# Second layer's expert results scattered by token tile by tile, residual rows and layernorm chains taken many heads early

## The chip, the cores and the metric

The kernel runs on one core of a Trainium2 chip. The metric is the device time of one execution in microseconds: 466.25 us is the median of three runs of the kernel before (465.55 to 466.74). The engines are TensorE (PE), VectorE (DVE), ScalarE (ACT), GpSimd (POOL) and SyncE (SP), each with its own in-order queue; they meet through semaphores.

## The reference

`x` is 1024 tokens of 256 channels (4 batches of 256), `ctx` has the same batches.

```python
x = x + xattn0(layernorm(x), ctx)     # activations per 1x128 and weights per 128x128 block
                                      # brought to an 8-bit grid, then x_q @ ctx_q.T
x = x + ffn0(layernorm(x), ...)       # 32 experts of width 192, top 4, softmax of the top, x 1.8,
                                      # plus one shared expert
x = x + xattn1(layernorm(x), ctx, gamma)  # 8 heads of 32 channels over 256 positions, softmax
x = x + ffn1(layernorm(x), ...)       # 8 experts of width 176, top 2, shares out of a full softmax,
                                      # plus a shared expert of width 352
```

## The kernel before, in words

Tokens lie in 8 tiles of 128 rows (`NT`), token tile t being `x_sb[:, t]`. Five parts follow one another.

**Start (0 to 49 us).** DVE takes the statistics of the layernorm, ACT normalises (L529 to L535). The context is scaled and rounded on DVE (L746 to L751) and POOL forms `wq` from it with one addition and one subtraction over 2048 columns (L436 to L438). DVE takes the largest value of each 128-block of the normalised x (L755), forms `rin_x` (L757 to L759), multiplies x by it (L761 to L763), and rounds in two halves (L769 to L773). PE multiplies, and DVE adds into `x_sb` (L778).

**First mixture of experts (layer m0, routing 49 to 94 us, tiles to 243.6 us).** The router chooses, one-hot matrices give each 128-row tile's list of tokens (`tab`), and for m0 also where each result row belongs (`dest`, L861 to L869: matmuls L1192, then `kth`). While the routing waits, ACT, POOL and PE work off four shared-expert steps (`early_shared`, `shared_steps`): POOL multiplies (L456) and adds the result to `x_sb` (L461), and DVE's tile loop begins only when all four are added (L923, L971). Then come 48 tiles of two 64-row blocks (`tiles`): POOL gathers rows (L482), ACT and DVE copy the second block's weights, PE does gate/up, transposes and down. POOL scatters each tile's rows to token-ordered homes in DRAM (`home`, L472), and SP loads them back, 512 KB for each token tile (L383).

**Second attention (243.6 to about 341 us).** `take(t)` adds the four weighted rows of each token of tile t into `x_sb` (L947, four operations in a chain). `queries(tiles)` then takes statistics and the reciprocal deviation on DVE, a chain of small linked operations (L303 to L313), scaled for the queries, and ACT normalises. The 32 heads go in 16 pairs, four heads to a token tile. PE does `scores` of a pair, DVE takes maxima (`head_max`, L979), ACT exponentiates (L646), PE turns the probabilities (`turn_p`, L1314), ACT copies them (L654), and after each tile's four heads PE does `values` (L1325, L1333), DVE `tile_out` (L990 to L994). PE's order is written out: turn pair p, scores of pair p+2, and for every second p the values of a tile. The orders on DVE and ACT are written out too: `takes` says before which head DVE takes which tile, `by_pair` at which head it makes which pair of tiles' queries, `by_pool` at which heads the deviation of the next layernorm goes to POOL (`deviations`), to be used by DVE three heads later.

**Second mixture of experts (m1: routing 341 to 366 us, tiles to 427.5 us).** The same with 20 tiles. SP stores every tile's result as it is (L351 to L353); at the end POOL gathers by token, 16 gathers for 8 token tiles and 2 choices (`gather_back`, L492), by way of the slots in `back` (L836).

**Last (427.5 us to the end).** Fifteen shared-expert steps remain (`after_shared`), and for the last eight DVE adds the routed rows (`combine`) and SP stores the output.

## Time and profile before

| | us |
|---|---|
| median of 3 runs | 466.25 |
| the profiled execution: device time | 468.48 |
| its span, first to last instruction | 466.4 |
| around the span (launch and end) | 2.08 |
| PE busy | 356.5 (76%) |
| DVE busy | 280.5 (60%) |
| ACT busy | 201.7 (43%) |
| POOL busy | 164.5 (35%) |
| mean granted clock of PE | 0.908 of full |

The shares are averages over parts with different limits. PE's granted clock is given as a share of full speed, 1.00 (2.4 GHz) or 0.50 (1.2 GHz); a mean between the two is a stretch with a change in it. "Issue" in the chain is time in which the engine waited for nothing that the profile shows.

### The profile page before, as it was taken

To read this page: it belongs to the slowest core of one execution; us is meant where nothing else is said; L and a number is where in the kernel's file an instruction comes from. 1 tells how busy PE (TensorE), PEld (TensorE's weight loads), DVE (VectorE), ACT (ScalarE), POOL (GpSimd) and SP (SyncE) were. 2 spreads that over 40 slices of the span, in tenths; PEclk is the share of its full clock that TensorE was granted. 3 is DMA by queue.
4 is the path that set the end of the run, shared out by engine and by line. 5 is a ranking of instruction groups with operands and counts; after the bars stand their busy time and mean duration, and the time that the engine had idled before them with its cause. 6 is when DMAs were issued, how large, how long until landed. Compare 5 with 4: busy or idle time off the path is not lost.

```text
span 466.4 us, 8276 instructions
## 1 busy us (share of the span) xinstructions
PE 356.5 (76%) x2359; PEld 203.0 (44%) x2359; DVE 280.5 (60%) x791; ACT 201.7 (43%) x467; POOL 164.5 (35%) x220
## 2 busy tenths in 40 slices
PE   0003397789999999999983665667766899998996
PEld 0002184435555545555442444444554345444664
DVE  3999859645555555555558639395877155554365
ACT  1301245255555555555413737355731355554221
POOL 2060204756666666666310000002310533300560
PEclk9999998999999999999995558596985699999999
DMA  8999970094222322345557930000002223321232
GB/s 236 353 302 271 341 192 0 23 298 128 91 91 91 91 92 92 92 106 172 164 183 296 272 107 3 0 1 0 4 3 88 69 91 92 94 68 45 80 114 79
DMA packets 28780, 57.32 MB, mean 123 GB/s; under 512 B 3825, under 2 KB 13937, under 8 KB 28737
## 3 DMA queue, kind: packets, MB, share of 16 engines
q1 hardware_dynamic: 20785, 38.38, 27.0%
q0 software_dynamic: 6336, 17.31, 12.7%
q10 hardware_dynamic: 1616, 1.11, 0.8%
q8 instruction: 21, 0.34, 0.3%
q14 instruction: 22, 0.18, 0.1%
HBM read 44.72 MB, written 12.06 MB: 122 GB/s over the span
## 4 chain that ended last, share of the span: by engine, by line
PE 66%; DVE 18%; issue 8%; ACT 3%; POOL 2%; DMA 2%; DVEq 0%; ACTq 0%; SPq 0%; POOLq 0%
PE bank L1226 19%; PE bank L1253 13%; PE bank L1100 5%; PE bank L1237 5%; PE bank L1302 4%; PE bank L1217 3%; PE bank L1111 3%; PE bank L1314 3%; PE bank L1151 2%; PE bank L1089 2%; DMA x_sb<-x 2%; DVE x_sb L947 1%; DVE att_nm L979 1%; PE bank L1333 1%; DVE st L704 1%
## 5 line engine op out<-in xcount | busy, mean ns | idle before, releaser
L1226 PE MATMUL bank<-arena,xT 128*64 x272 | 112.5, 496 | 1.3 <-ACT xT L608 1.3
L1229 PE MATMUL bank<-xn,xT 128*64 128x384 f32 (+1 forms) x272 | 112.5, 497 | 0.0
L482 POOL DMA_INDIRECT xg<-m_xn,tab x68 | 65.7, 967 | 61.3 <-PE bank L1217 52.5
L1253 PE MATMUL bank<-arena,hT 96*64 (+1 forms) x272 | 70.4, 381 | 1.9 <-DVE hT L906 1.3
L1256 PE MATMUL bank<-xn,hT 96*64 96x256 f32 (+1 forms) x272 | 70.4, 381 | 0.0
L601 ACT ACTIVATE xn<-arena 128x768 f32 (+1 forms) x68 | 56.3, 827 | 21.9 <-issue 21.8
L931 DVE TENSOR_TENSOR hh<-sg,bank 128x192 f32<-128x192 f32 (+1 forms) x71 | 24.8, 350 | 63.0 <-ACT sg L624 63.0
L474 POOL DMA_INDIRECT m_ys<-ysb,dest x48 | 47.4, 988 | 23.9 <-issue 12.8
L1253 PEld LDWEIGHTS bank<-arena,hT 96*64 96x64 f32 (+1 forms) x272 | 34.8, 135 | 38.7 <-issue 28.2
L608 ACT ACTIVATE xT<-bank 128x256 f32<-128x256 f32 x71 | 27.2, 383 | 47.8 <-PE bank L1217 47.1
L1302 PE MATMUL bank<-arena,xn 32*128 32x256 f32 x128 | 23.0, 521 | 27.7 <-issue 21.4
L900 DVE COPY xn<-arena 96x512 f32 (+1 forms) x68 | 28.8, 423 | 23.7 <-issue 23.7
L1226 PEld LDWEIGHTS bank<-arena,xT 128*64 128x64 f32 x272 | 31.8, 138 | 23.7 <-issue 14.6
L303 POOL TENSOR_SCALAR ve<-mv 128x2 f32<-128x2 f32 (+1 forms) x4 | 0.8, 194 | 110.1 <-DVE mv L707 110.1
L979 DVE TENSOR_REDUCE att_nm<-bank 128x2 f32<-128x512 f32 x32 | 21.4, 685 | 26.8 <-PE bank L1302 26.6
L624 ACT ACTIVATE sg<-bank 128x192 f32<-128x192 f32 (+1 forms) x71 | 23.2, 326 | 32.7 <-PE bank L1229 30.1
L918 DVE COPY ysb<-bank 128x256 f32<-128x256 f32 x68 | 28.9, 425 | 14.0 <-PE bank L1256 9.1
L646 ACT ACTIVATE arena<-bank,att_nm 128x256 f32<-128x256 f32 x64 | 29.7, 473 | 14.9 <-DVE att_nm L979 14.8
L1256 PEld LDWEIGHTS bank<-xn,hT 96*64 96x64 f32 (+1 forms) x272 | 34.8, 135 | 0.0
L1100 PE MATMUL bank<-arena 128*128 128x352 f32 (+1 forms) x84 | 33.2, 523 | 0.0
L1229 PEld LDWEIGHTS bank<-xn,xT 128*64 128x64 f32 x272 | 31.9, 138 | 0.0
L530 ACT ACTIVATE xn<-x_sb,nmr,rstd 128x256 f32<-128x256 f32 x24 | 12.7, 590 | 43.5 <-DVE nmr L740 35.2
(173 smaller groups left out, 615.2 us busy)
## 6 DMA issues: line engine op xcount, KB each, us to landing
arena<-w_gu SPq DMA_DIRECT2D x3, 3456.0 KB, 18.8
arena<-w_dn SPq DMA_DIRECT2D x3, 1728.0 KB, 24.5
arena<-m_ys SPq DMA_DIRECT2D x8, 512.0 KB, 5.5
m_ys<-ysb SPq DMA_DIRECT2D x20, 128.0 KB, 1.7
arena<-w_gu SPq DMA_DIRECT2D x2, 1056.0 KB
m_xn<-xn SPq DMA_DIRECT2D x2, 1024.0 KB, 6.4
arena<-w_gu SPq DMA_DIRECT2D x1, 1408.0 KB
arena<-w_gu SPq DMA_DIRECT2D x1, 1152.0 KB, 11.5
```

Source lines behind the costliest of these rows:

```text
L474: nc.gpsimd.indirect_dma_start(out=ys_d[L.name], out_offset=bass.IndirectOffsetOnAxis(ap=dest[:, s:s + 1], axis=0), in_=ysb[:, s % BUFS, : ...
L482: nc.gpsimd.indirect_dma_start(out=xg[:, b, :], out_offset=None, in_=xn_d[L.name], in_offset=bass.IndirectOffsetOnAxis(ap=d["tab"][:, s:s ...
L601: nc.scalar.activation(second[L.name][0][:, s % 2, :], arena[:, bass.ds(off, L.gu)], ACT.Copy).then_inc(m["gu_second"], 1)
L646: nc.scalar.activation(pr_sb[:, g % 4, q, :], bank[g % 4][:, q * H:(q + 1) * H], ACT.Exp, bias=nm[:, g % 4, q:q + 1], accum_out=sum_sb[:, ...
L900: V.tensor_copy(second[L.name][1], arena[0:L.J, bass.ds(off + L.gu, 2 * H)]).then_inc(m["dn_second"], 1)
L918: V.tensor_copy(ysb[:, s % BUFS, :], bank[6 + s % 2][:, 0:H]).then_inc(m["y_copied"], 1)
L1100: ins = T.matmul(bank[4 + n % 2][:, 0:2 * J2], RS[L.name]["xT"][:, t, c, :], arena[:, at:at + 2 * J2], start=(c == 0), stop=(c == C - 1))
L1226: T.matmul(bank[2 + s % 2][0:BLOCK, 0:2 * J2], xT[:, s % 2, c, 0:BLOCK], arena[:, bass.ds(off + c * 2 * J2, 2 * J2)], start=(c == 0), stop ...
L1229: return T.matmul(bank[2 + s % 2][BLOCK:P, 0:2 * J2], xT[:, s % 2, c, BLOCK:P], gu2[:, s % 2, cols], start=(c == 0), stop=(c == C - 1), ti ...
L1253: T.matmul(bank[6 + s % 2][0:BLOCK, 0:H], hT[0:L.J, s % 2, a, 0:BLOCK], arena[0:L.J, bass.ds(off + L.gu + a * H, H)], start=(a == 0), stop ...
L1256: ins = T.matmul(bank[6 + s % 2][BLOCK:P, 0:H], hT[0:L.J, s % 2, a, BLOCK:P], dn2[:, a * H:(a + 1) * H], start=(a == 0), stop=(a == 1), ti ...
L1302: ins = T.matmul(bank[g % 4][:, q * H:(q + 1) * H], xn[rows, t, q * P:(q + 1) * P], k_sb[rows, t, :], start=True, stop=True, tile_position ...
```

## The change

Four edits go together.

1. Start: the product x times `rin_x` moves from DVE to ACT, 16 operations of 128 columns; `wq` moves from POOL to DVE, its addition ahead of the rounding, its subtraction between the two halves.
2. Early shared steps: POOL does the multiplications only; its four additions into `x_sb` are made in the tile loop, one ahead of each of the gathers 4 to 7. ACT writes the four results to four buffers. DVE's tile loop waits for an addition only where it writes over that buffer.
3. Attention: tiles 0 and 1 have their queries made together, tiles 2 and 3 are taken before the first head, tiles 4 to 7 before heads 1, 2, 6 and 7. The deviations of the queries from tile 2 on, and of the next layernorm, are made by POOL: `chains` says at which head DVE gives the statistics, for which tiles, whether for queries, and at which head they are used.
4. Second layer: results go to token-ordered homes as in the first layer, with `kth`, `dest` and the matmuls for them, and are loaded back by SP. PE's tiles wait for `dest_ready`. The SP stores and the 16 gathers at the end go.

```diff
-        by_pair = {4: (2, 3), 12: (4, 5), 19: (6, 7)}
-        by_pool = {22: (0, 1), 24: (2, 3), 28: (4, 5)}
+        chains = [(-1, (2, 3), True, 2), (2, (4, 5), True, 7), (7, (6, 7), True, 12),
+                  (11, (0, 1), False, 15), (19, (2, 3), False, 23), (27, (4, 5), False, 31)]
@@ sync
-                    if L is L1:
-                        sp.dma_start(ys_d[L.name][s * P:(s + 1) * P, :],
-                                     ysb[:, s % BUFS, :]).then_inc(m["y_stored"][s % BUFS], 16)
...
             store_tiles(L1)
+            rows_of_tokens(L1)
@@ gpsimd
-            pool.wait_ge(c_mag, 1)
-            link(nc.gpsimd.tensor_tensor(v_c, v_c, c_c, ALU.add))
-            nc.gpsimd.tensor_tensor(wq.rearrange("p b k n -> p (b k n)"), v_c, c_c, ALU.subtract).then_inc(wq_ready, 1)
...
+            def early_add(L, n):
+                q, t = M[L.name]["early"], early_work[L.name][n][1]
+                pool.wait_ge(q["y_copied"], n + 1)
+                nc.gpsimd.tensor_tensor(x_sb[:, t, :], x_sb[:, t, :], ysb[:, n, :], ALU.add).then_inc(q["added"], 1)
...
                         pool.wait_ge(m["t_done"], s - BUFS + 1)
+
+                        if s - BUFS < n_early[L.name]:
+                            early_add(L, s - BUFS)
...
-                    if L is L0 and s >= ahead:
+                    if s >= ahead:
                         home(s - ahead)
...
             def deviations(i):
+                _, tiles, asked, _ = chains[i]
+                a, b = tiles[0], tiles[-1] + 1
                 pool.wait_ge(stats_ready, i + 2)
-                inverse_deviation(nc.gpsimd, link, by_pool[sorted(by_pool)[i]], 1.0)
-                pool.sem_inc(rstd_ready, 1)
+                inverse_deviation(nc.gpsimd, link, tiles, SCALE if asked else 1.0)
+                link(nc.gpsimd.tensor_tensor(nmr[:, a:b], mv[:, a:b, 0], rstd[:, a:b], ALU.mult))
+                nc.gpsimd.tensor_scalar(nmr[:, a:b], nmr[:, a:b], -1.0, None, ALU.mult).then_inc(rstd_ready, 1)
@@ scalar
+            act.wait_ge(rin_ready, 1)
+            for a in range(16):
+                block_of = v_x[:, a * P:(a + 1) * P]
+                nc.scalar.activation(block_of, block_of, ACT.Copy, scale=rin_x[:, a:a + 1]).then_inc(xs_ready, 1)
...
-            queries(1, [0])
-            softmax_exp(0)
-            softmax_exp(1)
-            queries(2, [1])
-            softmax_exp(2)
+            act.wait_ge(chain_ready, 1)
+            for t in range(2):
+                normalise(t, q_ready)
+            for g in range(3):
+                softmax_exp(g)
...
-                if g in by_pair:
-                    queries(3 + sorted(by_pair).index(g), by_pair[g])
+                for i, (_, tiles_of, asked, turn) in enumerate(chains):
+                    if asked and turn == g:
+                        act.wait_ge(rstd_ready, i + 1)
+                        for t in tiles_of:
+                            normalise(t, q_ready)
@@ vector
-            link(V.scalar_tensor_tensor(out=amx[:], in0=amx[:], scalar=ACT_EPS, in1=amx[:], op0=ALU.max, op1=ALU.max))
+            link(V.tensor_scalar(amx[:], amx[:], ACT_EPS, None, ALU.max))
             link(V.reciprocal(rin_x[:], amx[:]))
-            link(V.scalar_tensor_tensor(out=rin_x[:], in0=rin_x[:], scalar=FP8_MAX, in1=rin_x[:], op0=ALU.mult, op1=ALU.max))
-            n = NT * H // 2
-            for i in range(2):
-                v16 = v_x[:, i * n:(i + 1) * n].rearrange("p (a n) -> p a n", n=P)
-                V.tensor_tensor(v16, v16, rin_x[:, 8 * i:8 * i + 8].unsqueeze(2).broadcast_to([P, 8, P]), ALU.mult)
+            V.tensor_scalar(rin_x[:], rin_x[:], FP8_MAX, None, ALU.mult).then_inc(rin_ready, 1)
+
+            link(V.tensor_tensor(v_c, v_c, c_c, ALU.add))
...
+                dve.wait_ge(xs_ready, 8 * (i + 1))
                 link(power_of_two(c, v))
                 link(V.tensor_tensor(v, v, c, ALU.add))
                 V.tensor_tensor(qx[:, i * n:(i + 1) * n], v, c, ALU.subtract).then_inc(xq_ready, 1)
+                if i == 0:
+                    V.tensor_tensor(wq.rearrange("p b k n -> p (b k n)"), v_c, c_c, ALU.subtract).then_inc(wq_ready, 1)
...
             take(0)
-            queries([0])
             take(1)
-            head_max(0)
-            head_max(1)
-            queries([1])
-            head_max(2)
-            head_max(3)
-
-            takes = {3: 2, 4: 3, 9: 4, 12: 5, 16: 6, 19: 7}
+            queries([0, 1])
+            take(2)
+            take(3)
+            statistics(chains[0][1]).then_inc(stats_ready, 1)
+            for g in range(4):
+                head_max(g)
+
+            takes = {1: 4, 2: 5, 6: 6, 7: 7}
             for g in range(nheads):
                 if g in takes:
                     take(takes[g])
-                if g in by_pair:
-                    queries(by_pair[g])
-                if g in by_pool:
-                    statistics(by_pool[g]).then_inc(stats_ready, 1)
-                if g - 3 in by_pool:
-                    dve.wait_ge(rstd_ready, sum(k <= g - 3 for k in by_pool))
-                    normalise(by_pool[g - 3], M["m1"]["xn_ready"])
+                for i, (given, tiles_of, asked, turn) in enumerate(chains):
+                    if given == g:
+                        statistics(tiles_of).then_inc(stats_ready, 1)
+                    if turn == g and not asked:
+                        dve.wait_ge(rstd_ready, i + 1)
+                        normalise(tiles_of, M["m1"]["xn_ready"])
@@ tensor
             routing(L1, rw1, (w1_in, 96), 2)
+            pe.wait_ge(dest_ready, 2)
             tiles(L1)
```

`rows_of_tokens(L)` is the loop of L383 to L388 made for either layer: eight loads, each from the fifth on waiting for the one four before it.

## Rows read from the trace of the kernel before

**Rows 1.** The page: shares by engine of the chain that ended last.
```profile
PE 66%; DVE 18%; issue 8%; ACT 3%; POOL 2%; DMA 2%; DVEq 0%; ACTq 0%; SPq 0%; POOLq 0%
```

**Rows 2.** Stretches: length, engines' busy us (instructions), clock, DMA share, GB/s.
```profile
243.60:341.00 97.40, 58.70 (x484) 39.09 (x484) 63.77 (x188) 53.53 (x170) 8.74 (x42) 0.70 0.28 87
366.00:427.50 61.50, 58.90 (x401) 28.31 (x402) 30.23 (x81) 31.95 (x63) 16.81 (x18) 0.96 0.28 83
427.50:466.40 38.90, 33.89 (x140) 22.12 (x140) 19.30 (x48) 9.75 (x28) 15.15 (x16) 1.00 0.29 85
```

**Rows 3.** Chain of waits in order of time: start us, us, what.
```profile
251.59 0.70 DVE att_nm L979
...
264.41 7.69 issue
...
288.21 7.04 issue
...
312.48 5.58 issue
```

**Rows 4.** Timeline 0 to 60 us: start, us, engine, line, operation, count, idle before.
```profile
16.63 4.04 ACT L530 ACTIVATE xn<-x_sb,nmr,rstd 128x256 f32<-128x256 f32 x8 [11.84 <-DVE nmr L740]
...
22.18 4.50 POOL L437 TENSOR_TENSOR arena<-arena 128x2048 f32<-128x2048 f32 x1 [18.36 <-DVE arena L727]
24.33 2.39 DVE L757 SCALAR_TENSOR_TENSOR amx<-amx 128x16 f32<-128x16 f32 x1
...
26.76 4.50 POOL L438 TENSOR_TENSOR arena<-arena 128x2048 bf16<-128x2048 f32 x1
27.04 4.25 DVE L759 SCALAR_TENSOR_TENSOR rin_x<-rin_x 128x16 f32<-128x16 f32 x1
31.32 2.36 DVE L763 TENSOR_TENSOR xn<-xn,rin_x 128x1024 f32<-128x1024 f32 x2
...
34.31 0.69 DVE L726 TENSOR_SCALAR arena<-xn 128x1024 int32<-128x1024 int32 x1
...
35.76 1.23 DVE L772 TENSOR_TENSOR xn<-xn,arena 128x1024 f32<-128x1024 f32 x1
```

**Rows 5.** Timeline of DVE, 262 to 318 us: a take and a pair's queries.
```profile
265.94 1.99 DVE L947 SCALAR_TENSOR_TENSOR x_sb<-arena,rw,x_sb 128x256 f32<-128x256 f32 x4
267.97 0.75 DVE L704 BATCH_NORM_STATS2 st<-x_sb 128x6 f32<-128x256 f32 x2
...
269.04 0.17 DVE L303 TENSOR_SCALAR ve<-mv 128x2 f32<-128x2 f32 x1
...
271.21 0.16 DVE L740 SCALAR_TENSOR_TENSOR nmr<-mv,rstd 128x2 f32<-128x2 f32 x1
```

**Rows 6.** Stretches of the attention, columns as in Rows 2.
```profile
256.50:264.40 7.90, 7.90 (x32) 5.38 (x32) 3.51 (x7) 6.81 (x25) 0.00 (x0) 0.50 1.05 296
...
272.10:278.50 6.40, 6.40 (x48) 4.19 (x48) 1.29 (x2) 2.41 (x8) 0.00 (x0) 0.50 0.26 57
...
323.00:338.00 15.00, 12.02 (x132) 8.27 (x131) 10.95 (x29) 11.72 (x38) 6.88 (x33) 1.00 0.01 3
```

**Rows 7.** Timeline of PE: turned probabilities of the twelfth and sixteenth pair.
```profile
322.79 1.14 PE L1314 MATMUL bank<-ident,arena 128*128 128x128 f32 x8
...
336.49 1.09 PE L1314 MATMUL bank<-ident,arena 128*128 128x128 f32 x8
```

**Rows 8.** Timeline, last deviations on POOL and DVE behind them.
```profile
335.99 0.19 POOL L303 TENSOR_SCALAR ve<-mv 128x2 f32<-128x2 f32 x1 [3.13 <-DVE mv L707]
...
339.86 0.19 POOL L313 TENSOR_TENSOR rstd<-nt,rstd 128x2 f32<-128x2 f32 x1
340.21 0.73 DVE L712 TENSOR_SCALAR xn<-x_sb,mv,rstd 128x256 f32<-128x256 f32 x2 [2.19 <-POOLq L510]
```

**Rows 9.** The page: the scatter of the first layer, busy us, mean ns, idle before.
```profile
L474 POOL DMA_INDIRECT m_ys<-ysb,dest x48 | 47.4, 988 | 23.9 <-issue 12.8
```

**Rows 10.** One line of the kernel: ns min/median/max, first and last start.
```profile
L866 DVE SCALAR_TENSOR_TENSOR kth<-bank,kth x3: 207/207/208, 89.0 to 89.4; 128x48 f32<-128x48 f32 x3
```

More of the change, by code:

```diff
@@ L223, in mk_xattn_ffn @@
         xn_d = {L.name: nc.dram_tensor(L.name + "_xn", (n_tok, H), F32, kind="Internal").ap() for L in (L0, L1)}
-        homes = (n_tok + 1) * L0.K
-        ys_d = {L.name: nc.dram_tensor(L.name + "_ys", (L.tiles * P + (homes if L is L0 else 0), H), F32, kind="Internal").ap()
-                for L in (L0, L1)}
+        homes = (n_tok + 1) * max(L0.K, L1.K)
+        ys_d = {L.name: nc.dram_tensor(L.name + "_ys", (homes + L.tiles * P, H), F32, kind="Internal").ap() for L in (L0, L1)}
         batch_in = [sem(f"batch_in{b}") for b in range(NB)]
@@ L291, in mk_xattn_ffn @@
         n_early = {"m0": 4, "m1": 1}
+        assert max(n_early.values()) <= BUFS
         n_mid = {"m0": 1, "m1": 1}
@@ L364, in store_tiles, with rows_of_tokens @@
                     sp.wait_ge(m["y_stored"][b], 16 * (L.tiles // BUFS))
+            def rows_of_tokens(L):
+                for t in range(NT):
+                    if t >= 4:
+                        sp.wait_ge(*returned(L, t - 4))
+                    at = (t * P + 1) * L.K
+                    sp.dma_start(back_rows[L.name][:, t], ys_d[L.name][at:at + P * L.K, :].rearrange(
+                        "(p k) h -> p k h", k=L.K)).then_inc(returned(L, t)[0], 16)
             sp.wait_ge(ctxT_in, 16)
@@ L517, in _ @@
             gathers(L1)
-            gather_back(L1)
         @block.scalar
@@ L655, in pT_copy @@
                                      ACT.Copy).then_inc(pT_ready, 1)
-            def queries(n, tiles):
-                act.wait_ge(chain_ready, n)
-                for t in tiles:
-                    normalise(t, q_ready)
-            queries(1, [0])
-            softmax_exp(0)
-            softmax_exp(1)
-            queries(2, [1])
-            softmax_exp(2)
+            act.wait_ge(chain_ready, 1)
[3 more added lines that the diff above has]
+                softmax_exp(g)
             for g in range(nheads):
@@ L917, in y_copy @@
                         dve.wait_ge(m["y_stored"][s % BUFS], 16 * (s // BUFS))
+                    elif s < n_early[L.name]:
+                        dve.wait_ge(m["early"]["added"], s + 1)
                     V.tensor_copy(ysb[:, s % BUFS, :], bank[6 + s % 2][:, 0:H]).then_inc(m["y_copied"], 1)
@@ L922, in tiles @@
                 dve.wait_ge(m["table_e"], m["nth"])
-                dve.wait_ge(m["early"]["added"], n_early[L.name])
                 every_tile = L.tiles + len(last_work[L.name])
```

104 lines of the change are left out of this document (35 added, 69 removed).

## Prediction

> **What bounds the kernel now.** I read the shares of the chain that ended last first: PE holds 66% of it, DVE 18%, and 8% is "issue", time in which PE stood still for a reason the profile doesn't name [rows 1]. Then the busy times by stretch. The second layer's tiles are PE's (58.9 us busy of 61.5, clock 0.96), and so is the end (33.9 of 38.9, clock 1.00). The attention isn't: in 97.4 us PE is busy for 58.7, DVE for 63.8, ACT for 53.5, and the clock is 0.70 on average [rows 2]. The chain in order of time says where this goes: PE stands still for 7.69, 7.04 and 5.58 us, each time ahead of scores [rows 3]. DVE's timeline has the reason: a take of 1.99 us, then the queries' statistics and chain from 267.97 to 271.37, 3.4 us in which DVE takes no maxima and ACT has nothing to normalise [rows 5]. So the attention is bound by what the order on DVE puts in front of the scores.
>
> I write all times on the axis of the profile before, and shift at the end.
>
> **Start.** Two operations of 16 columns, L757 and L759, take 2.39 and 4.25 us on DVE. They end when POOL's L437 and L438 end (22.18 + 4.50 and 26.76 + 4.50) [rows 4]: while POOL worked, DVE stood. With `wq` off POOL they cost what small operations cost, about 0.2 each [rows 10]. Now step by step. The reduction has ended at 24.33; two small operations and a reciprocal bring `rin_x` at 25.0. DVE then adds for `wq` over 2048 columns, twice the 1.23 of 1024 columns: 27.5, and makes `dq`, 0.6: 28.1. ACT meanwhile scales 8 blocks. Eight normalisations of 256 columns took 4.04 [rows 4]; half the columns cost at most that and at least half. I take 3.0: 28.0, in time. The first half's rounding is 2 x 0.70 + 2 x 1.25 = 3.9: 32.0. Then the subtraction for `wq`, 2.4, and the second half, 3.9: 38.3, where before it ended at 42.1 (34.31 + 2 x 3.9). ACT's second eight blocks hide under this. **-3.8 us**. Bounds: -2.7 if a block costs a full 0.5 (8 blocks end at 29.1), -4.1 if everything small is free.
>
> **Early shared steps.** POOL's four additions leave the routing for the tile loop. POOL's multiplications come out of the order sooner only if an addition was in front of one. DVE's stretch there is busy with 16-bit comparisons, and it should lose less to POOL. I take **-0.3**, bounds -0.8 and 0. In the tile loop POOL does an addition ahead of each of four gathers; it has four buffers' lead there, and scatters begin only with the eighth tile. Cost 0; if DVE's copies are held each time for one addition (a 2048-column operation is 4.50 [rows 4], an eighth is 0.6) and nothing takes it up, +2.4.
>
> **Attention.** First maximum before: 251.59 [rows 3]. Changed, from 243.6: two takes 4.0, one chain for two tiles 3.4, two more takes 4.0, statistics 1.1 [rows 5]: 256.2. That is 4.6 us later. The first turned probabilities follow 1.7 us on (a maximum of 0.7 [rows 3], an exponential of about 1): 257.9. The first pairs have no values. Two such pairs took 7.90 us at clock 0.50, 32 matmuls [rows 6], so 3.95 each. Pairs 0 and 1 end at 265.8. During this DVE has takes 4 and 5, statistics and the maxima of the fourth pair to do (2.0 + 2.0 + 1.1 + 1.3), which cannot all be hidden: I give 1 us. With pair 2's turns and scores 270.8. Values and pair 3 are one stretch of 48 matmuls, 6.4 us at 0.50 [rows 6]: 277.2. Now DVE alone holds PE: a maximum 0.7, tile-out 1.4, take 2.0, statistics 1.1, a maximum 0.7 = 5.9 us (take 6 was hidden before). 283.1; values at the upper level, 1.5: the sixth pair is turned at 284.6.
> From here no take is left, the queries' chains run on POOL, and only light work stands on DVE. POOL's chain took 335.99 to 340.05 for 14 linked operations [rows 8], 0.29 each; 16 take 4.6 us. Chain 1 is given at head 2 and used at head 7, chain 2 given at 7 and used at 12: five heads of 1.7 us each, 8.5 us, so neither is waited for. The rate is that of the last stretch before, in which DVE had no takes either: twelfth pair at 322.79, sixteenth at 336.49 [rows 7], four pairs in 13.7 us, 3.4 a pair at clock 1.00. Ten pairs: 34.3. The sixteenth pair is turned at 318.9 instead of 336.5: **-17.6 us**. The same from the other side: three stalls of 20.3 go [rows 3], and with them two returns of the clock to 0.50 that cost some 3 each; the later start takes back 4.6, the new wait 3 to 4.
> Bounds: ten pairs at 3.1 and no wait at the sixth pair give -24; at 3.7, with the clock at 0.50 again after the wait, -11.
>
> **End of the attention.** DVE waited 2.19 us for POOL's last deviations, and the last tile's values behind it [rows 8]. Given at head 27 instead of 28 the chain begins about 1.4 earlier and is 0.55 longer: **-0.9**, bounds -1.5 and +0.5.
>
> **Second routing.** Added: eight matmuls of 20 columns (eight of 128 take 1.14 [rows 7]; I take 0.3) and three DVE operations in a chain, 0.21 each [rows 10]. One copy (`back`) goes. DVE's multiplication for the shared step is queued behind them, and PE's next transposes wait for it; the gather of the first tile, issued before, lands under this. **+0.5**, bounds 0.2 and 1.5. That `dest_ready` is waited for on PE costs no more, as DVE has `dest` 2 us before PE arrives there.
>
> **Second layer's tiles.** POOL now has a gather and a scatter for each tile: 2 x 0.99 [rows 9] and 0.3 of issue behind each, 2.6 us. A tile takes 61.5 / 20 = 3.1 us, fill included [rows 2]. It fits; the first layer runs so. 0, and +4 if the scatter's landing is waited for (0.2 a tile). SP's stores were hidden, so nothing is gained.
>
> **Last stretch.** The 16 gathers go and eight loads of 256 KB come. 2 MB at 296 GB/s [rows 6] are 7 us; from 431 they have landed by 438 to 440, and the first is wanted after eight of the sixteen steps' times, at about 447 (427.5 + 8 x 2.4). PE bounds it as before [rows 2]. 0.
>
> **Sum.** -3.8 - 0.3 - 17.6 - 0.9 + 0.5 = -22.1 us. The profiled execution took 468.48 us (span 466.4 and 2.08 around it), so 446.4 for such a one; it lies 2.2 above the median of 466.25, and on the median's footing the result is **444.2 us**.
>
> **Rivals.**
> *The clock falls back in the new wait.* My walk has PE idle for 3 to 4 us before the sixth pair. Against: nothing but a short wait, and pairs run dense before it. For: after the stalls of 7.04 and 5.58 PE began again at 0.50. A pair with values takes 6.4 there against 3.4 and 1.5, and two pairs pass until it rises: +3 to +3.5, and if it happens twice +6.5: 447.5 to 450.7. 25%.
> *The clock rises early.* What the rows show: in 256.5 to 264.4 PE is busy for 7.90 of 7.90 us and the clock stays at 0.50; in the next busy stretch, with values in it, it rises after 6.4 us [rows 6]. If it rose in the first pairs, pair 2, values and pair 3 would take about 6 us instead of 11.4; DVE would then be the bound and give back 1.8: 440.6. 12%. The Trainium skill ("TensorE: Matmul & The Clock Gate", Why this matters for your kernels) says to keep TensorE busy without gaps to get it past the slow state; by that rule this rival is the forecast, at 440.6. The busy 7.90 us at 0.50 here speak against it.
> *The stall only moves.* Takes, statistics or POOL's chains come late, DVE holds the scores for some 4 to 8 us more, or the scatters are waited for in the second layer: 448 to 452. 8%.
> *Slower.* The takes and the waits of ACT for POOL leave PE just enough gaps that it never leaves 0.50 between 244 and the second layer's tiles. Two pairs are then 3.95 + 6.4 = 10.4 us, ten pairs 52 instead of 34.3: +17.7; the end of the attention and the second routing add 4, the pairs before 2. -22.1 + 23.7 = +1.6: 467.9. It decides from nine pairs of ten on. Against: in all three busy stretches with values the clock rose. 5%.
> My own case has 50%.
>
> **Range and chances.** 8 in 10: from 438 (the attention's upper bound shared with the early rise) to 454. The measurement tells 0.3%, 1.4 us, from no change. Faster 0.94, the same 0.02, slower 0.04 (the slower case lies at the very edge, so a part of its 5% counts as the same).
>
> **What would show it.** L757's and L759's successors under 0.3 us, the rounding's end at 38; the first maximum 4 to 5 us later behind the last m0 tile; no stall over 5 us after it, and at most one of 3 to 4 before the values of the second tile; PE's clock over 0.85 in the attention's second half; POOL's chains without a wait on ACT; 20 tiles in 61 to 62 us with 20 scatters on POOL. I am wrong if the clock stays at 0.50 in the pairs from the sixth on, or if maxima wait behind something other than a take.

## The result, and the profile after

The changed kernel takes 452.44 us (median of 4 runs, 451.57 to 453.46) where the kernel before took 466.5 beside it: ratio 0.9694, 95% interval 0.9655 to 0.9732. Run again later beside the experiments it took 452.93 us, ratio 0.9673 (0.963 to 0.9715). The prediction was 444.2 us, the range 438 to 454. The direction and the place of the gain are right, its size is not: the profiled execution went from 468.48 to 452.69 us (span 450.4), 15.8 us where 22.1 were predicted. The other 2 of the 8 us are a matter of footing: the profile before lay 2.2 us above its median, the one after 0.25. The medians here and below are over all runs; the ratios leave out a run more than 1.5% above its kernel's fastest (one each of "takes spread" and "second layer's scatter undone" below).

The page's shares of the chain answer to [rows 1]. PE has gained a point, issue has fallen from 8% to 5%:
```profile
PE 67%; DVE 19%; issue 5%; ACT 3%; POOL 3%; DMA 2%; DVEq 0%; SPq 0%; ACTq 0%; POOLq 0%
```
Stretches of the changed kernel, with the columns of [rows 2]. The first is the attention (97.0 us from about the first take, about as long as before), the next two are the second layer's tiles and the last stretch:
```profile
241.00:338.00 97.00, 65.45 (x564) 44.84 (x564) 65.85 (x203) 56.26 (x176) 20.41 (x97) 0.77 0.32 99
350.00:411.50 61.50, 59.39 (x401) 28.35 (x401) 30.31 (x79) 31.95 (x63) 36.50 (x38) 0.95 0.27 83
411.50:450.40 38.90, 33.98 (x142) 22.17 (x140) 19.32 (x48) 9.75 (x28) 0.96 (x1) 0.97 0.26 85
```
The last two are what they were (58.90 and 33.89 us of PE before). In the first, PE does 564 matmuls where it did 484, at clock 0.77 instead of 0.70: the work is denser, and a part of the second routing's falls in it now.

The start, timeline (start, us, engine, line): the two small operations are free of GpSimd, and the rounding ends at 37.5 where it ended at 42.1:
```profile
23.89 0.17 DVE L739 TENSOR_SCALAR amx<-amx 128x16 f32<-128x16 f32 x1
24.38 0.17 DVE L741 TENSOR_SCALAR rin_x<-rin_x 128x16 f32<-128x16 f32 x1
24.59 4.78 ACT L522 ACTIVATE xn<-xn,rin_x 128x128 f32<-128x128 f32 x16 [4.36 <-DVE rin_x L741]
...
36.26 1.23 DVE L755 TENSOR_TENSOR ysb<-xn,arena 128x1024 bf16<-128x1024 f32 x1
```
They took 2.39 and 4.25 us in [rows 4], now 0.17 each. Their form has changed too, but one of the old form over 48 columns takes 0.21 [rows 10], so it is GpSimd's absence that counts.

The attention is where the rest lies. PE multiplies with the reciprocals of the softmax sums at the start of each tile's values. One line for each tile but the first, with the wait in front of it in brackets:
```profile
278.94 1.08 PE L1305 MATMUL bank<-ident,arena 128*32 128x128 f32 x16 [3.61 <-DVE arena L968]
288.74 0.64 PE L1305 MATMUL bank<-ident,arena 128*32 128x128 f32 x16 [1.75 <-DVE arena L968]
296.49 0.64 PE L1305 MATMUL bank<-ident,arena 128*32 128x128 f32 x16 [0.77 <-DVE arena L968]
303.92 0.64 PE L1305 MATMUL bank<-ident,arena 128*32 128x128 f32 x16 [1.42 <-DVE arena L968]
312.70 0.64 PE L1305 MATMUL bank<-ident,arena 128*32 128x128 f32 x16 [1.48 <-DVE arena L968]
320.13 0.64 PE L1305 MATMUL bank<-ident,arena 128*32 128x128 f32 x16 [2.48 <-DVE arena L968]
325.04 0.64 PE L1305 MATMUL bank<-ident,arena 128*32 128x128 f32 x16 [1.95 <-DVE arena L968]
```
No stall of 5 to 8 us is left, of which there were three [rows 3]; in their place stands a wait of 0.8 to 3.6 us in every tile, 13.5 us in seven. Each time it is for the reciprocal on DVE (L968). The sixteenth pair is turned at 321.56 instead of 336.49 [rows 7]. (A pair counts from the start of its first turn.)

Why DVE is late with them is seen in the chain of waits, in order of time (start us, us, what), from the second scores of a tile on:
```profile
283.63 1.32 PE bank L1282 x8
284.95 0.67 DVE att_nm L961
285.62 0.40 DVE arena L972
286.05 0.43 DVE arena L974
286.50 0.44 DVE x_sb L976
286.96 0.76 DVE st L687 x2
...
288.49 0.20 DVE arena L968
```
At step 10 of its loop DVE gets the scores of head 14 at 284.95, takes one maximum (L961), then writes out the tile before (L972 to L976), takes statistics (L687), takes another maximum, and only then forms reciprocals (L968) whose sums had long been there. It had itself been idle for 4.89 us ahead of that maximum, waiting for PE. The two engines wait for each other in turn.

The clock, over the wait at 278.94 and over the ten pairs behind it:
```profile
276.00:284.00 8.00, 5.06 (x42) 3.40 (x44) 3.90 (x11) 3.87 (x14) 3.19 (x16) 0.57 0.01 3
281.70:321.60 39.90, 30.81 (x317) 20.70 (x313) 22.19 (x54) 29.21 (x98) 8.72 (x44) 0.93 0.00 1
```
It did fall back in the new wait, to 0.50 from 277 to 284, and once more from 304.5 to 307.9. A second profile of the same kernel (the run "changed, again" below) has the first fall too (279.5 to 282.9), but then two others, 289.7 to 293.2 and 320.5 to 323.9, and none at 304. Its ten pairs took 38.7 us.

Second routing, added operations: three of 0.18 us on DVE. PE waits 0.94 us for DVE's multiplication behind them (0.52 before), but later 0.54 us for the first tile's gather to land, so the gather sets the time:
```profile
346.32 0.18 DVE L845 SCALAR_TENSOR_TENSOR kth<-bank,spare 128x20 f32<-128x20 f32 x1
...
346.75 0.18 DVE L850 SCALAR_TENSOR_TENSOR dest<-bank,kth 128x20 uint32<-128x20 f32 x1
346.85 0.33 DVE L861 TENSOR_TENSOR hh<-sg,bank 128x176 f32<-128x176 f32 x1
...
350.03 0.66 PE L1197 MATMUL bank<-ident,xg 128*128 128x128 f32 x2 [0.54 <-DMA xg<-m_xn,tab]
```

### The profile page after: what moved, and what is told of

Its sections match the earlier page's. It is cut to its first block, busy times and chain, and to the rows that moved or that the text cites. A ratio compares the mean times of both kernels' runs of the same rounds, so it can differ in the third digit from the quotient of the medians.

```text
span 450.4 us, 8288 instructions
## 1 busy us (share of the span) xinstructions
PE 354.4 (79%) x2367; PEld 202.0 (45%) x2367; DVE 267.2 (59%) x745; ACT 205.7 (46%) x483; POOL 168.0 (37%) x276
## 4 chain that ended last, share of the span: by engine, by line
PE 67%; DVE 19%; issue 5%; ACT 3%; POOL 3%; DMA 2%; DVEq 0%; SPq 0%; ACTq 0%; POOLq 0%
PE bank L1206 21%; PE bank L1233 13%; PE bank L1081 6%; PE bank L1217 5%; PE bank L1092 4%; PE bank L1197 4%; DVE x_sb L930 3%; PE bank L1294 2%; PE bank L1282 2%; PE bank L1132 2%; DVE st L687 2%; DVE att_nm L961 2%; DMA x_sb<-x 2%; PE bank L1070 1%; PE bank L1313 1%
## 5 line engine op out<-in xcount | busy, mean ns | idle before, releaser
L466 POOL DMA_INDIRECT m_ys<-ysb,dest x68 | 67.0, 986 | 38.8 <-DVE ysb L902 22.0
L914 DVE TENSOR_TENSOR hh<-sg,bank 128x192 f32<-128x192 f32 (+1 forms) x71 | 24.8, 349 | 62.4 <-ACT sg L609 62.4
L593 ACT ACTIVATE xT<-bank 128x256 f32<-128x256 f32 x71 | 27.2, 384 | 47.9 <-PE bank L1197 47.8
L609 ACT ACTIVATE sg<-bank 128x192 f32<-128x192 f32 (+1 forms) x71 | 23.2, 327 | 32.7 <-PE bank L1209 30.2
L961 DVE TENSOR_REDUCE att_nm<-bank 128x2 f32<-128x512 f32 x32 | 20.7, 673 | 23.4 <-PE bank L1282 22.1
L1217 PEld LDWEIGHTS bank<-ident,hh 128*96 128x96 f32 (+1 forms) x142 | 12.2, 125 | 41.0 <-issue 37.9
L1217 PE MATMUL bank<-ident,hh 128*96 128x128 f32 (+1 forms) x142 | 29.8, 292 | 0.3 <-DVE hh L914 0.3
```

The source lines that it names most:

```text
L466: nc.gpsimd.indirect_dma_start(out=ys_d[L.name], out_offset=bass.IndirectOffsetOnAxis(ap=dest[:, s:s + 1], axis=0), in_=ysb[:, s % BUFS, : ...
L961: V.tensor_reduce(nm[:, g % 4, :], bank[g % 4][:].rearrange("p (q k) -> p q k", q=2), AX.X, ALU.max, negate=True).then_inc(nm_ready, 1)
L1217: ins = T.transpose(bank[4 + s % 2][0:L.J, a * P:(a + 1) * P], hh[:, s % 2, a * L.J:(a + 1) * L.J], ident[:])
```

## Experiments

Each is the changed kernel with one edit (the last two rows join several), timed five to ten times beside the kernel before. Differences to the changed kernel are taken between ratios (its own is 0.9673) times 468 us. An interval is about 0.4% to either side, that of a difference about 0.6%, 2.2 to 3.2 us. So five lines differ clearly from the changed kernel: start, attention, chains on DVE, the two edits together and, barely, the last. Against its first measurement, 0.9694, every difference would read 1.0 us lower.

The last column has the attention's length in the one profile of each, from the first take to the last normalisation. It leaves out what happens before and behind, and in the five profiles with an unchanged attention (the first two rows, additions, scatter and the first profile) it lies between 90.4 and 92.2 us.

| kernel | median us | ratio (95%) | to the changed one, us | attention, us |
|---|---|---|---|---|
| changed, again | 452.93 | 0.9673 (0.963 to 0.9715) | | 90.4 (first profile 91.2) |
| start undone | 458.11 | 0.978 (0.9753 to 0.9806) | +5.0 | 91.8 |
| attention's order undone | 464.54 | 0.9919 (0.9886 to 0.9952) | +11.5 | 103.4 (kernel before 104.7) |
| additions undone | 451.21 | 0.963 (0.9608 to 0.9652) | -2.0 | 91.7 |
| second layer's scatter undone | 453.27 | 0.9667 (0.9631 to 0.9703) | -0.3 | 92.2 |
| chains on DVE, early takes kept | 460.72 | 0.9858 (0.9816 to 0.9901) | +8.7 | 98.4 |
| filler ahead of the values | 450.18 | 0.962 (0.9584 to 0.9657) | -2.5 | 90.1 |
| filler ahead of the attention | 451.95 | 0.9647 (0.9619 to 0.9674) | -1.2 | 91.7 |
| reciprocals early | 450.60 | 0.964 (0.96 to 0.968) | -1.5 | 89.1 |
| takes spread | 450.23 | 0.9607 (0.9554 to 0.966) | -3.1 | 87.7 |
| reciprocals early, takes spread | 448.81 | 0.9586 (0.9549 to 0.9622) | -4.1 | 85.8 |
| both, and additions undone | 450.41 | 0.9617 (0.959 to 0.9644) | -2.6 | 86.4 |

### Which part brings what

**The changed kernel again.**

> The changed kernel itself once more, beside which the other experiments are to be read. On its first chip its ratio to the kernel before was 0.9694 (0.9655 to 0.9732). If that holds here: 0.967 to 0.971; the variants with one part undone would then read as +4.0 us (start), +10.5 (attention), -3.0 (additions) and -1.3 (scatter). If the ratio is lower on other chips (0.963 to 0.966), the last two are no difference, start and attention are worth 1 to 3 us more each, and the reciprocals moved alone and the filler are worth little.

Its ratio is 0.9673, between the two cases. The additions and the scatter are then within the error, start and attention are worth 5.0 and 11.5 us. The four parts undone add up to 14.2 us, the whole change is worth 15.3 on the same footing.

**The start undone.**
```diff
+ link(nc.gpsimd.tensor_tensor(v_c, v_c, c_c, ALU.add))
+ nc.gpsimd.tensor_tensor(wq..., v_c, c_c, ALU.subtract)
- nc.scalar.activation(block_of, block_of, ACT.Copy, scale=rin_x[:, a:a + 1])
+ V.tensor_tensor(v16, v16, rin_x[...].broadcast_to([P, 8, P]), ALU.mult)
```


> The changed kernel with the start as before: the conversion of ctxT (add and subtract over 2048 columns) on GpSimd again, no scaling by ACT, scaling by DVE. Theory (the start was worth 4.6 us by the traces, and 2.0 us of that were lost again in the first routing, because TensorE's clock fell there to 0.50 at another place): 452.4 + 2 to 4.6 = 454.5 to 457.0 us; the two 16-column operations on DVE take 2 to 4.5 us again, the first expert tile begins some 3 us later. If the clock does not fall at the gate matmuls here, the time is at the low end, 454.5 to 455.5, and the 2.0 us belong to the start's new timing. Rival (the 2.0 us come from the moved additions and would be lost with the old start too): 456.5 to 457.0, and the stretch from the rounding's end to the first expert tile is as long as in the changed kernel (about 53 us).

+5.0 us, so the start is worth what its trace shows (4.6), within the error. The two operations take 2.39 and 4.25 us again. The first expert tile's first matmul comes at 95.39 us, 4.8 later than in the changed kernel's first profile (90.58); the low end of the theory is out, and so is that the new timing of the start costs 2 us. The rival's sign is met, 53.6 us from the rounding's end to the first expert tile; whether the additions are the reason is the next experiment's question.

**The additions undone.**
```diff
- if s - BUFS < n_early[L.name]: early_add(L, s - BUFS)
...
+ nc.gpsimd.tensor_tensor(x_sb[:, t, :], x_sb[:, t, :], ysb[:, (n - 1) % 2, :], ALU.add)   # in early_shared
```


> The changed kernel with the early shared steps' additions in the first and second routing again (on GpSimd between its multiplications), not in the tile loop. In the traces so far the stretch from the first counting matmul to the first expert tile is 22.9 us with these additions (kernel before) and 24.3 to 24.8 without them (three kernels), though DVE's one-hot operations are faster without. Theory 1 (moving the additions costs: without them TensorE's gate matmuls of the shared steps follow at another time and stand at clock 0.50 longer, up to 2.77 us for a set that takes 1.46 otherwise): this kernel is faster than the changed one by 1 to 2 us, 450.5 to 451.5, the stretch 22.5 to 23.2 us. Theory 2 (the clock falls there from run to run whatever the order): 452.0 to 453.0, the stretch about 24.3. Theory 3 (my prediction, the move gains 0.3): 452.7.

Theory 1 fails in the trace: the stretch from the counting matmul (66.46) to the first expert tile (90.77) is 24.3 us with the additions back, not 22.5 to 23.2. Theory 2 stands as to the stretch, though the time, 451.21 us, is theory 1's. The sets of four gate matmuls take 1.46 us or up to 2.77, nearly twice that. In two profiles of the same changed kernel they are, first profile and then second:
```profile
68.70 2.48 PE L1081 MATMUL bank<-arena 128*128 128x384 f32 x4
74.01 1.46 PE L1081 MATMUL bank<-arena 128*128 128x384 f32 x4
```
```profile
69.44 2.76 PE L1081 MATMUL bank<-arena 128*128 128x384 f32 x4
74.71 2.77 PE L1081 MATMUL bank<-arena 128*128 128x384 f32 x4
```
Over all profiles of the changed kernel and its variants the stretch is 23.2, 24.3 or 24.8 us, in the kernel before 22.9; with the additions back it was 24.3 once and 23.2 once, so their place doesn't decide it. (The granted clock's own row reads 1.00 from 70 to 80 us in the second profile, so that the clock slows them there isn't shown.) By its ratio this kernel is 2.0 us faster than the changed one, but the intervals overlap, and in the last experiment the same edit brought nothing.

**The second layer's scatter undone.**
```diff
+ if L is L1: sp.dma_start(ys_d[L.name][s * P:(s + 1) * P, :], ysb[:, s % BUFS, :])
+ nc.gpsimd.indirect_dma_start(out=back_rows[L.name][:, t, k, :], ..., in_=ys_d[L.name], ...)   # 16, behind the last tile
- home(s), rows_of_tokens(L1), kth and dest for L1
```


> The changed kernel with the second layer's results stored tile by tile by SP and gathered back for each token, as before (no scatter, no kth and dest in the second routing, 16 gathers behind the last tile). Theory (by the traces the second routing changed by 0.0, the tiles by +0.2 and the combination by nothing, because TensorE is the bound of the last stretch and the gathers were in time): 452.4, from 451.7 to 453.0. Rival (the scatters cost in the tiles what the saved gathers bring at the end, or the other way round, by 1 us): 451 or 453.5.

-0.3 us: no difference, though the rival's 1 us either way would not show. In the traces the tiles take 56.6 us without the scatter and 57.2 with it, and the last stretch 43.2 in both (43.2 and 44.8 in the changed kernel's two profiles): PE bounds both stretches that this part touches.

**The attention's order undone.**
```diff
- takes = {1: 4, 2: 5, 6: 6, 7: 7}
+ takes = {3: 2, 4: 3, 9: 4, 12: 5, 16: 6, 19: 7}
...
+ if g in by_pair: queries(by_pair[g])               # by_pair = {4: (2, 3), 12: (4, 5), 19: (6, 7)}
```


> The changed kernel with the order of the attention as before (tokens taken at heads 3, 4, 9, 12, 16, 19, the queries' chains on DVE in front of maxima, GpSimd's three chains late). Theory (the attention is where the gain is: 12.3 us to the last turned pair and 1.1 at its end): 452.4 + 13.4 = 465.8 us, 464.5 to 467, and three stalls of TensorE of 5 to 8 us ahead of scores are back. Rival (part of the gain comes from the earlier start or from nothing in the order, for instance from where the clock happens to rise): 458 to 462.

+11.5 us, somewhat less than the 13.4 of the traces. The three stalls are back (7.69, 7.04 and 5.34 us in its chain), and with them the low clock, the fives in the middle of this line (a digit for each fortieth of the span, in tenths of full speed):
```profile
PEclk9999998899999999999995569586976799999998
```
Its ten runs lie from 461.95 to 468.21 us, and the one profiled took 462.91, so its trace shows the order's cost at the low end.

**The early takes kept, the chains back on DVE.**
```diff
- statistics(tiles_of).then_inc(stats_ready, 1)          # chain follows on GpSimd
...
+ link(statistics(tiles_of)); inverse_deviation(V, link, tiles_of, SCALE); negated_means(...)
```


> The changed kernel with the queries' chains of tiles 2 to 7 (three times some 2.5 us of small linked operations) on DVE again, at the same heads, with the early takes kept: so only GpSimd's share of the change is taken away. Theory (both count: the early takes put the work ahead of and into the first pairs, the chains on GpSimd keep 2.4 us out of each of three places on DVE; at the start of the attention and at heads 2 and 7 nothing hides them): +2.4 for the first maximum, and 2.4 to 3 more at the take of tile 7, where TensorE already waits 3.6 us: in all 5 to 7 us slower than the changed kernel. Rival (the early takes alone are the gain, since DVE has slack in the first pairs at clock 0.50): 1 to 3 us slower, the first maximum late by 2.4 and the rest hidden.

+8.7 us, above the theory's 5 to 7 by less than the error, and far from the rival. In its trace the first maximum comes 2.4 us later behind the first take (14.96 against 12.59), and the whole attention takes 98.4 us, 7.2 to 8.0 more than in the changed kernel's two profiles. PE's wait ahead of the sixth pair, 3.61 us in the changed kernel, is now:
```profile
285.31 1.08 PE L1311 MATMUL bank<-ident,arena 128*32 128x128 f32 x16 [6.29 <-DVE arena L968]
```
So of the 11.5 us in the attention most hangs on the chains that GpSimd has taken over; the early takes alone bring about 3, hardly more than the error (5.0 in the last column of the table, 103.4 against 98.4). Late takes with the chains on GpSimd were not run, so how far the two need each other is open. A linked operation costs GpSimd 0.29 us and DVE 0.20, and it still pays: PE, DVE and ACT wait for one another in a ring of scores, maxima, exponentials and turns, and GpSimd stands outside it.

### Why a pair takes 4.0 us and not 3.4

**Reciprocals one head earlier.**
```diff
- if g % HPT == HPT - 1: head_inverses(g // HPT)
+ if g % HPT == HPT - 2: head_inverses(g // HPT)     # ahead of tile_out
```


> The changed kernel, only the reciprocals of a tile's sums stand one head earlier on DVE: ahead of the third head's tile-out, take and statistics and not behind them. Theory (the ten pairs took 4.0 us and not 3.4 because TensorE waits for these reciprocals before each tile's values, 13.5 us in seven waits; behind them ACT is next, with 2 x 0.47 + 2 x 0.2 for the exponentials and 0.6 for a copy, 1.75 a head, 3.5 a pair): ten pairs in 35 to 36.5 us, 452.4 - 4 = 448.5, from 447.0 to 449.5; TensorE's waits for the reciprocals fall under 4 us in all and the clock does not fall in the second half. Rival 1 (the ring of scores, maxima, exponentials and turns is what sets the pace, the reciprocals only end a wait that would be there anyway): the waits move to the turns, ten pairs stay at 39 to 40 us, 451.5 to 452.5. Rival 2 (the clock): the same time as far as it still falls twice.

The waits for the reciprocals are gone altogether (13.5 us to 0), yet the time falls by 1.5 us only, which the error covers, and the ten pairs took 39.8 us. Theory and rival 1 are each right in half: a part of the wait has moved. The sixteenth pair does come 3.6 us earlier (317.99 against 321.56, though this execution's first take was 0.9 later); at the last normalisation 1.3 is left of it (330.94 against 332.21), as DVE waits 1.60 us for GpSimd's last chain, which starts only 1.3 us earlier. The chain of waits of this kernel:
```profile
278.19 0.50 DVE x_sb L930
278.70 0.76 DVE st L687 x2
...
279.66 0.67 DVE att_nm L961
...
281.37 0.50 ACT arena L639
...
282.00 0.63 PE bank L1294 x4
282.63 1.83 PE bank L1282 x8
284.46 1.90 PE bank L1294 x8
```
The take of tile 7 (L930) and its statistics stand ahead of a maximum (L961), on which an exponential and the turn (L1294) depend. PE waited 3.17 us there, and then worked at 0.50 to 293: eight transposes in 1.90 us, 1.10 at the upper level.

**Takes spread over the tiles**, alone and with the reciprocals early.
```diff
- takes = {1: 4, 2: 5, 6: 6, 7: 7}
+ takes = {1: 4, 3: 5, 9: 6, 13: 7}
- chains: (2, (4, 5), True, 7), (7, (6, 7), True, 12)
+ chains: (3, (4, 5), True, 8), (13, (6, 7), True, 18)
```


> The changed kernel with the takes of tiles 5, 6 and 7 at heads 3, 9 and 13, the reciprocals where they are. Theory (two things hold TensorE between the fifth and the sixteenth pair, the reciprocals behind tile-out and takes, and the two takes in a row at heads 6 and 7): the wait ahead of the sixth pair falls from 3.6 to under 2 us and the clock does not fall there, but TensorE still waits 1 to 2.5 us ahead of each tile's values: ten pairs in 37.5 to 39, 1.5 to 2.5 us faster than the changed kernel and 2 to 3 slower than with the reciprocals moved too. Rival (the takes are all of it): as fast as with both, 3.5 to 4 faster than the changed kernel. Third (the reciprocals are all of it): no faster than the changed kernel, since the takes now stand in front of the reciprocals at head 9 to 11.

> The changed kernel with the reciprocals one head earlier (as in the run before this) and the takes of tiles 5, 6 and 7 and their statistics at heads 3, 9 and 13 instead of 2, 6 and 7. With the reciprocals alone moved, TensorE no longer waited for them, but for exponentials (3.17 us ahead of the sixth pair's second head), since the maximum stood behind tile-out, two takes and statistics, and the clock was 0.50 for 9 us behind that wait. Theory (the wait follows what DVE has to do in one tile; with one take a tile DVE has under 6.5 us of work per tile of 7 us, and TensorE no wait over 1.5 us, so the clock stays up): ten pairs at 3.5 to 3.6, the sixteenth pair 3.5 to 5 us earlier than with the reciprocals alone, ratio 0.954 to 0.957 of the kernel before. Rival (ACT and the ring of maxima, exponentials and turns hold the pair at 3.9 whatever DVE's order): ratio 0.962 to 0.965. Third (the takes now meet the maxima later, and one stall comes at the eighth or tenth pair): 0.958 to 0.962 with a clock fall there.

Alone 3.1 us faster than the changed kernel, between theory and rival, just inside the error; together 4.1, so the reciprocals add about 1 us and not 2 to 3. Together they are the one faster variant whose interval stands clear of the changed kernel's. The attention in the profiles agrees: 89.1 and 87.7 us with one edit, 85.8 with both, against 90.4 and 91.2. It is the third case of the expectation (0.958 to 0.962), and its clock fall came as well: PE waits 1.92 us for ACT within the ninth pair, and the clock is 0.50 from 290.2 to 293.6:
```profile
289.09 0.63 PE L1294 MATMUL bank<-ident,arena 128*128 128x128 f32 x4 [1.92 <-ACT arena L639]
```
The sixth pair comes at 276.04 (before 281.66) and the sixteenth at 312.99 (321.56): 8.6 us earlier, and 7.9 with the first layer's earlier end taken off. The ten pairs took 36.9 us, 3.7 a pair; behind that fall, from the twelfth to the sixteenth, it is 12.35 us for four (300.64 to 312.99), 3.1 a pair. There ACT is the busiest, 13.98 us of 16 against 13.51 on PE and 11.25 on DVE, and PE's waits end with ACT's copies. The stretch 296 to 312, first the changed kernel (its second profile), then this one:
```profile
296.00:312.00 16.00, 11.86 (x130) 7.83 (x128) 10.67 (x27) 11.91 (x41) 3.19 (x16) 1.00 0.01 2
```
```profile
296.00:312.00 16.00, 13.51 (x152) 8.95 (x155) 11.25 (x27) 13.98 (x48) 3.20 (x16) 1.00 0.01 2
```
Half of the 8 us is given back. At the attention's end DVE waits longer for GpSimd's last chain (1.59 us, 1.04 in the changed kernel),
```profile
317.78 0.41 DVE L695 TENSOR_SCALAR xn<-x_sb,mv,rstd 128x256 f32<-128x256 f32 x1 [1.59 <-POOL nmr L493]
```
and the last normalisation comes 6.1 us earlier, not 8.6 (326.13 against 332.21). Then, between the second layer's last tile and the shared steps, the clock fell, and for longer than in the changed kernel. The changed kernel's first profile, its second, then this one:
```profile
410.45 0.42 PE L1233 MATMUL bank<-arena,hT 88*64 x1 [1.35 <-DVE hT L888]
...
411.46 1.45 PE L1081 MATMUL bank<-arena 128*128 128x352 f32 x4
```
```profile
409.13 0.64 PE L1233 MATMUL bank<-arena,hT 88*64 x1 [1.34 <-DVE hT L888]
...
410.99 2.24 PE L1081 MATMUL bank<-arena 128*128 128x352 f32 x4
```
```profile
405.45 0.43 PE L1233 MATMUL bank<-arena,hT 88*64 x1 [1.69 <-DVE hT L888]
...
406.58 2.71 PE L1081 MATMUL bank<-arena 128*128 128x352 f32 x4
```
From the last gate/up matmul to the end it is 43.2, 44.8 and 46.3 us. So the fall is not this variant's own; but in all three profiles with the takes spread this stretch takes 46.3 to 47.9 us, in all others 43.2 to 44.8, and whether the new timing brings that or chance isn't shown. The six runs of this variant are 447.4 to 447.7 us three times, at a mean granted clock of 0.931 to 0.932, and 450.0 to 452.4 three times, at 0.919 to 0.923. The slower half thus ran at a lower clock; where it fell is known for the profiled one alone.

**Filler ahead of the values.**
```diff
+ if 1 <= t < NT - 1:
+     for _ in range(8): T.transpose(bank[6 + t % 2][:, H:H + P], ident[:], ident[:])
  pe.wait_ge(inv_ready, t + 1)
```


> The changed kernel with eight additional transposes of the identity on TensorE ahead of the values of tiles 1 to 6, into a part of the bank that the next matmuls overwrite: TensorE works where it waited for the reciprocals. Theory (order on DVE): the clock no longer falls at 277 and 304 us, which gives back some 2.5 us at the first place (values 3.0 instead of 1.7, turns 2.0 instead of 1.1) and 1 at the second, but the waits for the reciprocals stay, so the pair stays near 3.8 and the time is 449 to 451. Rival (the clock alone made 4.0 out of 3.4): 446.5 to 448.5. Third (the filler is itself in the way where the wait was under 1.1 us, and the clock falls all the same): 452.4 to 455.

450.18 us is the theory's time, but -2.5 us is within the error. The waits for reciprocals fell to 7.4 us since the transposes fill them; the clock still fell ahead of the sixth pair, and between it and the sixteenth not at all, where the changed kernel's two profiles have one and two falls. Ten pairs took 37.6 us instead of 39.9 and 38.7. So keeping the clock up behind the sixth pair is worth 1 to 2 us up to the sixteenth pair; of that little is left at the attention's end (90.1 us against 91.2 and 90.4).

**Filler ahead of the attention.**
```diff
+ pe.wait_ge(M["m0"]["y_copied"], every_m0)
+ for _ in range(52): T.transpose(bank[7][:, H:H + P], ident[:], ident[:])
  scores(0)
  scores(1)
+ for _ in range(26): T.transpose(bank[7][:, H:H + P], ident[:], ident[:])
```


> The changed kernel with transposes of the identity on TensorE where it stands idle ahead of the attention: 52 of them behind the first layer's last tile (241.0 to 248.5 us at the upper clock) and 26 behind the first scores (250.3 to 254). Theory (the clock is 0.50 in the first pairs because TensorE stood idle for 9.2 and 3.8 us before them; at the upper clock the first five pairs are bound by DVE and ACT, which have 3.5 us of work a pair): the sixth pair is turned 2.5 to 4 us earlier, 452.4 - 3 = 448.5 to 450.5. Rival 1 (DVE with its four takes bounds that stretch whatever the clock): 451.5 to 452.5, the wait ahead of the sixth pair grows by what is gained before it. Rival 2 (the transposes run at 0.50 and come in the way of the scores): 453 to 456.

This is the prediction's rival "the clock rises early", made true. Stretches 256 to 264 and 264 to 272 of the changed kernel (second profile), then of this one:
```profile
256.00:264.00 8.00, 8.00 (x35) 5.49 (x34) 4.41 (x10) 5.69 (x22) 1.79 (x9) 0.50 1.05 280
264.00:272.00 8.00, 6.89 (x50) 4.02 (x49) 6.32 (x15) 5.43 (x18) 3.71 (x16) 0.50 0.74 213
```
```profile
256.00:264.00 8.00, 4.68 (x33) 3.04 (x32) 5.74 (x13) 6.98 (x24) 1.66 (x9) 0.98 1.05 284
264.00:272.00 8.00, 7.87 (x60) 5.10 (x60) 4.88 (x12) 5.04 (x18) 3.72 (x16) 0.59 0.76 222
```
The first pairs do run at 0.98 instead of 0.50, PE needs 4.68 us for what took 8.00, and the values of the first tile come only 1.6 us earlier (267.15 against 268.71): DVE's takes of tiles 4 and 5 stand between its maxima, ACT comes late behind them (PE's longest wait, 2.61 us ahead of 264.13, ends with a copy of ACT), and the clock is down again by 264. The time is -1.2 us, no difference that this measurement can tell, and the attention is no shorter (91.7 us). Rival 1 holds in its time; its sign doesn't, as the wait ahead of the sixth pair did not grow (3.61 us).

**Both edits, and the additions undone.**
```diff
- if g % HPT == HPT - 1: head_inverses(g // HPT)
+ if g % HPT == HPT - 2: head_inverses(g // HPT)
- takes = {1: 4, 2: 5, 6: 6, 7: 7}
+ takes = {1: 4, 3: 5, 9: 6, 13: 7}
- early_add(L, s - BUFS)
...
```

> The changed kernel with the reciprocals one head earlier, the takes of tiles 5 to 7 at heads 3, 9 and 13, and the early shared steps' additions back in the routings. With the first two alone the ratio was 0.9586 (0.9549 to 0.9622), with the additions alone 0.963 (0.9608 to 0.9652) against 0.9673 (0.963 to 0.9715) of the changed kernel. Theory (moving the additions into the tile loop costs some 2 us, on top of everything): 0.9545 and in any case under 0.9565. Rival (the additions make no difference, and the 0.4% lay in where the clock falls from one execution to the next): 0.9575 to 0.9600.

0.9617: it lies above the theory's bound and above the rival's, and it isn't faster than without the third edit (0.9586, intervals overlapping). Here the additions undone read 1.5 us slower, alone they read 2.0 faster: no difference that could be told. The lowest ratio is that of the two edits in the attention.

## Why the prediction was right and where it wasn't

- **Start.** -3.8 predicted, -4.6 in the trace (0.4 of it is x landing earlier), 5.0 by the experiment. Right. ACT's blocks took 0.30 us each, not 0.375.
- **Early shared steps.** -0.3 predicted, no difference by two experiments. The trace after shows 1.3 us lost there, in gate matmuls that took up to 2.5 us instead of 1.46; which of them are slow changes from profile to profile.
- **First maximum.** 4.6 us later relative to the first take, as predicted (12.6 against 8.0). Sixth pair turned 41.0 us after that take, measured 40.7, with the wait of 3 to 4 us ahead of it (3.61) for the reason given: take, statistics and maximum on DVE.
- **Ten pairs at 3.4 us.** This is the step that failed: "The rate is that of the last stretch before, in which DVE had no takes either", 34.3 us. It took 39.9, 4.0 a pair, 5.6 us more (38.7 in the second profile). The last stretch before wasn't free of waits (its 13.7 us for four pairs hold two, of 0.55 and 2.01 us, for the same reciprocals), but it held no fall of the clock, and DVE came into it with a lead. I took the rate of a stretch without asking what was in it. In the changed kernel the waits behind the sixth pair are 7.9 us and two spells at 0.50 come on top. How much is which: in the second profile four pairs (299.04 to 313.62) ran at clock 1.00 with these waits and took 14.6 us, 3.65 a pair. So about half of the excess is the waits and the rest the clock. The experiments put the waits down to DVE's order and not to any engine's load: with reciprocals moved and takes spread the ten pairs take 3.7 each, and the last four of them 3.1. My own sign of being wrong, maxima that wait behind something other than a take, came true: they stand behind tile-out and statistics.
- **Rival "the clock falls back in the new wait".** 447.5 to 450.7, given 25%. The fall came as described, at that place, and a second one at 304. Its price was estimated at 3 to 6.5; with the filler behind the sixth pair's fall the ten pairs were 1.1 to 2.3 us shorter. Together with the waits of "the stall only moves" (448 to 452, 8%) it describes what happened better than my own case. I had set the two against each other, but they are one thing: short waits in every tile, behind some of which the clock fell.
- **Rival "the clock rises early".** Forced by filler it brings 1.2 us, not 3.6. By the rule of the Trainium skill ("TensorE: Matmul & The Clock Gate", Why this matters for your kernels) the engine should be kept busy to reach the upper level. The trace agrees that this works (0.98 instead of 0.50). It also shows that nothing measurable is gained by it where another engine sets the pace.
- **End of the attention** -0.9, measured -1.1. **Second routing** +0.5, measured 0: PE's wait for DVE is 0.4 us longer, about as predicted, but the gather's landing hides it. **Tiles** 0, measured +0.2, and **last stretch** 0, measured 0; the experiment without the scatter agrees within its error.

So by the first pair of traces 6.3 us are missing: 5.3 in the attention up to the sixteenth pair (-12.3 instead of -17.6, all of it the ten pairs' rate), 1.5 in the start and first routing together (-2.6 instead of -4.1), and 0.5 the other way in what follows.

## What to carry to other kernels

When a rate is carried over from a stretch of the old trace, take it apart first into work and waits: the waits don't come along unless the order behind them does. The order on the engine that feeds TensorE can matter where its load doesn't: 13.5 us of waits ended with reciprocals of 0.2 us. But a wait is not a gain: with all of them gone the kernel was 1.5 us faster, with the heavy items in the row spread as well 4.1, since other waits took their place. Here small linked chains were better off on an engine outside the ring, though it takes half as long again over them.

## What the runs showed of the hardware

The granted clock falls behind some short waits and not behind others, and one kernel does either. In the changed kernel's two profiles TensorE waited 2.48 us for the same reciprocals (at 320.13 and at 319.61): the clock stayed at 1.00 in one and was 0.50 from 320.5 on in the other. Ahead of the second layer's last matmuls it held behind a wait of 1.35 us, and in the second profile it was 0.50 from 409.2 on behind one of 1.34; the last stretch took 43.2 and 44.8 us. A part of a gain in one stage can so be lost in a later one that the edit didn't touch, and a single profile can't tell an edit of this size.

Executions of one kernel lie up to 6 us apart (449.9 to 454.0, 447.4 to 452.4, 461.95 to 468.21). In the second of these the slower three have the lower mean clock, 0.919 to 0.923 against 0.931 to 0.932. In the third they don't (0.908 to 0.919 above 465 us, 0.912 to 0.919 below), so something besides the clock spreads the runs there, and no run shows what.

Two operations of 16 columns on DVE took 2.39 and 4.25 us while GpSimd worked on 2048 columns for 4.50, and 0.17 each without it; with GpSimd's work put back they took 2.39 and 4.25 again.
